# One graph-network kernel, one edit: the running maxima are subtracted by VectorE instead of by a matrix product, and the weighting runs two steps behind the scores

## What is computed

```python
for i in range(NUM_BLOCKS):                      # 4
    y = _cond_layer_norm(x, cond, ...)
    # _sparse_attention, H = 4 heads of Dh = 128
    q = (x @ wq + bq).reshape(N, H, Dh) * Dh ** (-0.5)
    k = (x @ wk + bk).reshape(N, H, Dh)
    v = (x @ wv + bv).reshape(N, H, Dh)
    scores = jnp.einsum('ehd,ehd->eh', q[src], k[dst])
    smax = jax.ops.segment_max(scores, src, num_segments=N)
    ex = jnp.exp(scores - smax[src])
    denom = jax.ops.segment_sum(ex, src, num_segments=N)
    attn = ex / denom[src]
    out = jax.ops.segment_sum(attn[:, :, None] * v[dst], src, num_segments=N)
    x = x + (out.reshape(N, D) @ wo + bo)
    ...                                          # conditional norm and perceptron
```

## Time and profile before

| | us |
|---|---|
| median of 3 runs | 3189.87 |
| lowest and highest run | 3188.07, 3192.56 |
| the profiled execution, its own time | 3188.7 |
| its span (first to last instruction) | 3186.9 |
| PE busy in it | 2920.2 (92%) |
| DVE busy | 1862.6 (58%) |
| POOL busy | 898.7 (28%) |
| ACT busy | 793.4 (25%) |

### The profile page before, as it was taken

How to read it: one execution, slowest core, us unless ns; L and a number is a source line. 1 busy time by engine, 2 the same in 40 slices (tenths; PEclk the granted TensorE clock), 3 DMA queues, 4 the chain that set the end, 5 groups by cost and what they waited for, 6 DMA issues and landing times.

```text
span 3186.9 us, 32021 instructions
## 1 busy us (share of the span) xinstructions
PE 2920.2 (92%) x11830; PEld 1894.8 (59%) x11830; DVE 1862.6 (58%) x3327; ACT 793.4 (25%) x1145; POOL 898.7 (28%) x730
## 2 busy tenths in 40 slices
PE   5878899999899999899999899999967799899999
PEld 1345567776457776457777456777534456566555
DVE  9999755556734555855554765554765788503111
ACT  1154442223112223112222212222221212213221
POOL 6632413344113343223333222334420500000100
PEclk9989899999999999999999999999988899999999
DMA  3000110001400000400000410000253144101001
GB/s 80 17 7 1 40 53 0 27 1 44 119 20 1 1 27 34 114 21 14 1 27 14 116 40 14 1 27 1 92 142 102 40 131 140 56 4 63 14 1 33
DMA packets 69063, 133.70 MB, mean 42 GB/s; under 512 B 10804, under 2 KB 11195, under 8 KB 68908
## 3 DMA queue, kind: packets, MB, share of 16 engines
q1 hardware_dynamic: 63372, 119.62, 12.7%
q0 software_dynamic: 5536, 12.03, 1.2%
HBM read 120.70 MB, written 10.92 MB: 41 GB/s over the span
## 4 chain that ended last, share of the span: by engine, by line
PE 76%; DVE 13%; DMA 4%; DVEq 2%; issue 2%; ACT 1%; POOLq 1%; POOL 1%; SPq 0%; ACTq 0%
PE ps L1504 12%; PE ps L1616 10%; PE ps L1731 9%; PE ps L1760 9%; PE ps L1495 7%; PE ps L1658 4%; PE ps L1589 3%; PE ps L1604 3%; PE ps L1606 3%; PE ps L1607 3%; PE ps L1605 3%; PE ps L1457 2%; PE ps L1752 2%; PE ps L1521 2%; DVE onehot_src L895 2%; DMA lite_ring<-in_basis 2%
## 5 line engine op out<-in xcount | busy, mean ns | idle before, releaser
L687 POOL TENSOR_TENSOR pacc<-pacc,prob 125x628 f32<-125x628 f32 (+1 forms) x288 | 406.5, 1411 | 381.4 <-DVE prob L1024 381.4
L1504 PE MATMUL ps<-yT,w 128*128 128x416 f32 (+1 forms) x1152 | 437.3, 536 | 18.8 <-DVE qk_lo L961 11.6
L970 DVE CUSTOM_DVE_ANT_0 ps<-ps,typed 125x628 f32<-125x628 f32 x320 | 260.2, 824 | 234.0 <-PE ps L1589 233.5
L1616 PE MATMUL ps<-prob,big 125*128 125x314 f32 x1280 | 392.5, 428 | 4.6 <-DVE prob L1024 4.6
L1327 ACT ACTIVATE prob<-ps 125x628 f32<-125x628 f32 x320 | 221.9, 693 | 630.9 <-PE ps L1607 630.9
L1760 PE MATMUL ps<-pieces,counts_r 125*125 125x512 f32 x1400 | 353.8, 407 | 1.7 <-DVEq L1120 1.6
L1504 PEld LDWEIGHTS ps<-yT,w 128*128 128x128 f32 x1152 | 225.9, 198 | 204.9 <-issue 193.1
L1024 DVE SCALAR_TENSOR_TENSOR prob<-prob,typed 125x628 f32<-125x628 f32 x320 | 260.0, 812 | 122.7 <-ACT prob L1327 122.7
L1760 PEld LDWEIGHTS ps<-pieces,counts_r 125*125 125x125 f32 x1400 | 257.1, 186 | 79.3 <-issue 17.4
L1604 PE MATMUL ps<-qk_hi 128*125 128x314 f32 x640 | 293.9, 459 | 0.1
L1616 PEld LDWEIGHTS ps<-prob,big 125*128 125x128 f32 x1280 | 228.2, 190 | 60.5 <-DVE prob L1024 9.2
(11 more groups left out here) (207 smaller groups left out, 4602.1 us busy)
## 6 DMA issues: line engine op xcount, KB each, us to landing
lite_ring<-in_basis SPq DMA_DIRECT2D x120, 256.0 KB, 2.7
basis<-in_basis SPq DMA_DIRECT2D x120, 256.0 KB, 2.6
w<-in_m_w SPq DMA_DIRECT2D x8, 1024.0 KB, 6.7
w<-in_wk SPq DMA_DIRECT2D x5, 1024.0 KB, 5.5
oT<-in_cw SPq DMA_DIRECT2D x9, 512.0 KB, 6.2
w<-in_wv SPq DMA_DIRECT2D x4, 1024.0 KB, 5.9
w<-in_wq SPq DMA_DIRECT2D x4, 1024.0 KB, 6.5
w<-in_wo SPq DMA_DIRECT2D x4, 1024.0 KB, 5.5
```

The source lines that it names most:

```text
L687: nc.gpsimd.tensor_tensor(pacc[:, c0:c0 + nn], pacc[:, c0:c0 + nn], prob[:, n % 3, p0:p0 + nn], ALU.add).then_inc(psum_done, 1)
L970: V.tensor_tensor_reduce(out=score_ps(s.slot), in0=score_ps(s.slot), in1=in_quarters(mneg[:, t, c0:c0 + HALF]), scale=1.0, scalar=-BIG, op ...
L1504: last = mm(lin_ps(job, 128, nn), weight[:, k, m * 128:(m + 1) * 128], lhs[:, k, c0:c0 + nn], start=(k == 0), stop=(k == KD - 1))
L1616: last = mm(o_halves[:, b, :], vrow[:, t, h * DH:(h + 1) * DH], prob[:, n % 3, b * QUARTER:(b + 1) * QUARTER], start=(t == 0), stop=(t == ...
```

## The change

Steps of the weighting pass are divided in two kinds. In "subtracted" steps (all of head 3, the lower steps of heads 1 and 2, and every other step, with j odd, of the rest) the fourth product of each quarter is left out, and a new DVE instruction (`shift_scores`, a TENSOR_TENSOR) adds minus the maxima to the tile while it moves it from PSUM to `prob`. ACT then takes the exponential in place in `prob`. There are 10 such steps in head 0, 15 each in heads 1 and 2, and 20 in head 3: 60 of 80 per block, 240 in all.

For that, minus the maxima must stand in every row: `max_row` now multiplies with `nmx[:, t]` broadcast to 125 columns, so that its product has 125 equal rows, and ACT copies 125 rows instead of 1 into `shift` (before: `mrow`). The steps that keep the fourth product use a matrix whose first row alone is ones.

DVE does `shift_scores` of step j + 1 at the head of its step j, ahead of `masked_max`, of the product with the counts and of `add_out`. PE weights step j - 2 instead of j - 1 in step j. A slot of a subtracted tile is free when DVE has shifted it (`shifted`).

```diff
--- before.py
+++ after.py
@@ -175,6 +175,18 @@
 SCORES = {(s.kind, s.h, s.j): s for s in plan_scores()}
 SCORES_PER_BLOCK = len(SCORES)
 EXPS = MAXES = HEADS * 2 * T
+
+
+def subtracted(h, j):
+    return h == HEADS - 1 or (h > 0 and j < T) or j % 2 == 1
+
+
+SHIFT_NO = {}
+for _h in range(HEADS):
+    for _j in range(2 * T):
+        if subtracted(_h, _j):
+            SHIFT_NO[_h, _j] = len(SHIFT_NO) + 1
+SHIFTS = len(SHIFT_NO)
 
 
 def build(nc, a, out):
@@ -292,6 +304,7 @@
         hi_ready = sem("hi_ready")
         score_full = sem("score_full")
         exp_done = sem("exp_done")
+        shifted = sem("shifted")
         max_done = sem("max_done")
         neg_max_ready = sem("neg_max_ready")
         prob_ready = sem("prob_ready")
@@ -398,14 +411,14 @@
         junk = pacc[:].bitcast(F16)[:, 0:N]
         cw = sl("cw", [128, 4, D], F32R)
         stage = oT[:, 0:2 * D].rearrange("p (a d) -> p a d", d=D)
-        mrow = sl("mrow", [128, N], F32R)
+        shift = sl("shift", [P, N], F32R)
         bcol = sl("bcol", [128, 3, KD], F32)
         mxp = sl("mxp", [P, T, 2], F32)
         nmx = sl("nmx", [P, T], F32R)
         mx = sl("mx", [P, T], F32)
         ident_r = sl("ident_r", [P, P + 1], F32R)
         rden = sl("rden", [P, T], F32)
-        ones_r = sl("ones_r", [128, 128], F32R)
+        first_row = sl("first_row", [P, P], F32R)
         att.close()
         keep.close()
 
@@ -875,12 +888,12 @@
 
             dve.wait_ge(edge_placed, EC)
             V.tensor_copy(es[:].rearrange("p a s -> p (a s)"), o_ps[:, 0:2 * SLOTS])
-            V.memset(ones_r[:].bitcast(F32), 1.0)
-            V.memset(mrow[:].bitcast(F32), 0.0)
+            V.memset(first_row[:].bitcast(F32), 0.0)
             V.memset(condS[:, N:N + 2].bitcast(F32), 0.0)
             V.memset(ident_r[:].bitcast(F32), 0.0)
             V.drain()
             V.tensor_copy(ident_r[:, 0:P], ident[0:P, 0:P])
+            V.memset(first_row[0:1, :].bitcast(F32), 1.0)
             V.drain().then_inc(blk_done, 1)
 
             for g in range(GROUPS):
@@ -1011,13 +1024,29 @@
                     V.scalar_tensor_tensor(out=x[:, t, :], in0=lin_ps(job, P, D), scalar=rden[:, t:t + 1],
                                            in1=x[:, t, :], op0=ALU.mult, op1=ALU.add).then_inc(lin_empty[job.slot], 1)
 
+                def shift_scores(h, j):
+                    s, n = SCORES["exp", h, j], h * 2 * T + j
+                    c0 = HALVES[j // T]
+                    dve.wait_ge(score_full, at(i, SCORES_PER_BLOCK, s.n + 1))
+                    if n >= 3:
+                        dve.wait_ge(pv_done, at(i, EXPS, n - 2))
+                        dve.wait_ge(psum_done, at(i, EXPS, n - 2))
+                    V.tensor_tensor(in_quarters(prob[:, n % 3, :]), score_ps(s.slot),
+                                    in_quarters(shift[:, c0:c0 + HALF].bitcast(F32)), ALU.add).then_inc(shifted, 1)
+
                 for h in range(HEADS):
                     if h == 1:
                         dve.wait_ge(xbias_done, at(i, 2, 1))
+                    for job in g["mrow"][h][-2:]:
+                        dve.wait_ge(lin_empty[job.slot], job.emptied)
                     for j in range(2 * T):
 
                         n = h * 2 * T + j
                         t, c0, nn = j % T, HALVES[j // T], HALF
+                        if j == 0 and subtracted(h, 0):
+                            shift_scores(h, 0)
+                        if j + 1 < 2 * T and subtracted(h, j + 1):
+                            shift_scores(h, j + 1)
                         if h + 1 < HEADS:
                             masked_max(h + 1, j)
                         dve.wait_ge(exp_done, at(i, EXPS, n + 1))
@@ -1286,8 +1315,8 @@
                     for n, job in enumerate(g["mrow"][h]):
                         t0, t1 = 4 * n, min(4 * n + 4, T)
                         act.wait_ge(lin_full, job.full)
-                        A.activation(mrow[0:1, t0 * P:t1 * P].rearrange("o (t n) -> o t n", n=P),
-                                     lin_ps(job, 1, (t1 - t0) * (P + 1)).rearrange("o (t n) -> o t n", n=P + 1)[:, :, 0:P],
+                        A.activation(shift[:, t0 * P:t1 * P].rearrange("o (t n) -> o t n", n=P),
+                                     lin_ps(job, P, (t1 - t0) * (P + 1)).rearrange("o (t n) -> o t n", n=P + 1)[:, :, 0:P],
                                      ACT.Copy).then_inc(lin_empty[job.slot], 1)
 
                 def copy_o(h, half):
@@ -1320,11 +1349,17 @@
                 for h in range(HEADS):
                     for j in range(2 * T):
                         s, n = SCORES["exp", h, j], h * 2 * T + j
-                        act.wait_ge(score_full, at(i, SCORES_PER_BLOCK, s.n + 1))
-                        if n >= 3:
-                            act.wait_ge(pv_done, at(i, EXPS, n - 2))
-                            act.wait_ge(psum_done, at(i, EXPS, n - 2))
-                        A.activation(in_quarters(prob[:, n % 3, :]), score_ps(s.slot), ACT.Exp, scale=DH ** -0.5).then_inc(exp_done, 1)
+                        if subtracted(h, j):
+                            act.wait_ge(shifted, at(i, SHIFTS, SHIFT_NO[h, j]))
+                            scores = prob[:, n % 3, :]
+                        else:
+                            act.wait_ge(score_full, at(i, SCORES_PER_BLOCK, s.n + 1))
+                            if n >= 3:
+                                act.wait_ge(pv_done, at(i, EXPS, n - 2))
+                                act.wait_ge(psum_done, at(i, EXPS, n - 2))
+                            scores = score_ps(s.slot)
+                        to = prob[:, n % 3, :] if subtracted(h, j) else in_quarters(prob[:, n % 3, :])
+                        A.activation(to, scores, ACT.Exp, scale=DH ** -0.5).then_inc(exp_done, 1)
                         if j == T:
                             copy_o(h, 0)
                     if h + 2 < HEADS:
@@ -1577,7 +1612,10 @@
                         if b.kind == "max":
                             pe.wait_ge(max_done, at(i, MAXES, b.h * 2 * T + b.j + 1))
                         else:
-                            pe.wait_ge(exp_done, at(i, EXPS, b.h * 2 * T + b.j + 1))
+                            if subtracted(b.h, b.j):
+                                pe.wait_ge(shifted, at(i, SHIFTS, SHIFT_NO[b.h, b.j]))
+                            else:
+                                pe.wait_ge(exp_done, at(i, EXPS, b.h * 2 * T + b.j + 1))
 
                 def max_scores(h, j):
 
@@ -1603,8 +1641,9 @@
                         o = score_ps(s.slot)[:, b, :]
                         mm(o, hi[:, 1, rows], hi[:, 0, cols], start=True, stop=False)
                         mm(o, hi[:, 1, rows], lo[:, 0, cols], start=False, stop=False)
-                        mm(o, lo[:, 1, rows], hi[:, 0, cols], start=False, stop=False)
-                        last = mm(o, ones_r[:, 0:P], mrow[:, cols], start=False, stop=True)
+                        last = mm(o, lo[:, 1, rows], hi[:, 0, cols], start=False, stop=subtracted(h, j))
+                        if not subtracted(h, j):
+                            last = mm(o, first_row[:], shift[:, cols], start=False, stop=True)
                     last.then_inc(score_full, 1)
 
                 def weighted_values(h, j):
@@ -1625,7 +1664,7 @@
                         tiles = range(4 * n, min(4 * n + 4, T))
                         for t in tiles:
 
-                            last = mm(lin_ps(job, 1, P + 1, (t - 4 * n) * (P + 1)), nmx[:, t:t + 1], ident_r[:],
+                            last = mm(lin_ps(job, P, P + 1, (t - 4 * n) * (P + 1)), nmx[:, t:t + 1].to_broadcast([P, P]), ident_r[:],
                                       start=True, stop=True)
                         last.then_inc(lin_full, 1)
 
@@ -1665,14 +1704,15 @@
                             if j == 0:
                                 projected(h + 1)
                             max_scores(h + 1, j)
-                        if j:
-                            weighted_values(h, j - 1)
+                        if j >= 2:
+                            weighted_values(h, j - 2)
                         if h and j < T:
                             if j == 0:
                                 pe.wait_ge(o_copied, at(i, 2 * HEADS, 2 * h))
                                 if h == 1:
                                     pe.wait_ge(w_in[0], at(i, 32, 32))
                             attended(h - 1, j)
+                    weighted_values(h, 2 * T - 2)
                     if h + 2 < HEADS:
                         project(h + 2, 0)
                     weighted_values(h, 2 * T - 1)
```

## The result

The changed kernel takes 3497.57 us (median of 4 runs, 3486.52 to 3543.48) against 3191.22 for the kernel before. One execution, the 3543 us one, was slow: TensorE's granted clock stood at 0.949 in it where it is otherwise 1.00 (0.915 in the mean, against 0.960 to 0.963), and it is left out of the ratio, 1.0945 [1.0919, 1.097]. Run again unedited (e1_again) it took 3488.39 (3486.70 to 3496.15), a ratio of 1.0935 [1.0917, 1.0953]. The forecast was 3476.

A forecast was written before the change was run, and what follows sets the result against it. PE, 76% of the chain, bounds the kernel, streaming unbroken in attention. Per block, waits for DVE net of savings add 71.8 us (head 0 16.6, heads 1 and 2 45.6 - 0.5, head 3 8.5, `max_row` 1.6): 3188.7 + 287 = 3476 us, range 3425 to 3525.

The forecast's parts named there:

- PE waits for the maximum in 152 steps: Heads 0 to 2, before the maximum scores: 152 PE gaps of about 1.95 us, some 295 us in all.
- Periods: Attention steps: lower steps of heads 1 and 2 5.02 us instead of 3.37; head 3 lower 4.28, upper 2.04.
- Pairs: Two steps with one shift, head 0 and upper steps of heads 1 and 2: 6.66 us instead of 5.00.
- Head 3's output products: Head 3's lower steps: PE waits for the output sum queued behind the shift, 32 gaps of about 1.5 us.
- What goes, 69 us: 240 steps lose two products of 0.144 us each: 69 us of PE time, a gain if DVE answered in time.
- `max_row`, 6 us: Ten products per head load 125 columns instead of 1: 0.4 us per head, 6 us in all.
- The lag: PE weighting two steps behind the scores: no wait forecast for it; a weighting moved into head 2's end gap gives -0.5 us.
- head 0's: Head 0's share of a block's sum: ten pairs at 1.66 us, 16.6 us, before its max_row share.
- such spells: Extra half clock at the heads' ends, 0 to 2 spells per block: up to 14 us more, in the range only.
- rival 1: TensorE's clock falls in every second of 46 waits per block: 161 us more, 3637 us; chance 0.05.
- rival 2: Head 3 does not wait, its output sums come in time: 32 steps less 1.5 us, 3428 us; chance 0.04.
- rival 3: PE never waits for DVE, so the 69 us become a gain: 3120 us; chance 0.03.

The follow-up runs named there:

- e2: The changed kernel with the maximum of step j put ahead of the shift of step j + 1 on DVE: 3299.11 us, ratio 1.0331.
- e4: The changed kernel with both maximum and output sum ahead of the shift in DVE's queue: 3166.67 us, ratio 0.9925 to the kernel before.
- e3: The changed kernel with the output sum of step j - 1 ahead of the shift, the maximum still behind it: 3440.45 us, ratio 1.0786.
- e7: The kernel before without the fourth product in the same 240 steps and nothing in its place: 3125.55 us, ratio 0.9792.
- e8: The kernel before with only the 125 equal rows of max_row added: 3198.1 us, ratio 1.0018.
- e5: The kernel before with only the lag: PE weights two steps behind the scores instead of one: 3222.07 us, ratio 1.0096.
- e12b: The changed kernel with only ACT's copy of the output's first half one step later: 3497.08 us, ratio 1.095.
- e10b: The changed kernel with maximum and output sum ahead of the shift, and ACT's copy of the output's first half one step later: 3171.23 us, ratio 0.9936.

## Why the prediction was right

- **PE waits for the maximum in 152 steps: right in place, count and size.** 295 us were forecast and 296.5 measured, in 152 waits. The step that carries the forecast, DVE's order at a point where both engines need each other, is proved by e2 and e4: the order alone is worth 189 us, and 322 with the output sum's.
- **Periods.** Lower steps of heads 1 and 2: 5.02 forecast, 5.02 and 5.03 measured. Pairs: 6.66 and 1.53 + 5.16 = 6.69. Head 3 lower 4.28 forecast and 4.27 measured, upper 2.04 and 2.03 to 2.05. The new instruction took 0.81, and 0.73 to the next start, as read from the maximum. The estimate from the Trainium skill ("Perfetto Trace Analysis", Optimizing Scalar/DVE Operations) was 0.78 from start to start; the trace has 0.73 here too.
- **Head 3's output products.** Right: in its lower steps PE waits for L1024, as in this timeline of PE in block 0, and e3 removes this wait alone: 48 us, as 32 gaps of 1.5 us had been forecast.

```profile
767.90 1.22 PE L1655 MATMUL ps<-prob,big 125*128 125x314 f32 x4
770.34 1.12 PE L1697 MATMUL ps<-w,oT 128*125 128x512 f32 x2 [1.23 <-DVE x L1024]
```

- **What goes, 69 us.** 66 by e7.
- **`max_row`, 6 us.** Partly luck. e8 measured 6, but the wide products themselves cost 0.27 us a head, 4 us in all, and longer spells of half clock the rest. Their busy time grew as bounded: 27.0 us for the 160 against 18.5.
- **The lag was costed at nothing, and that was wrong by itself.** It costs 30 us alone (e5), 20 of them through ACT's queue, which I had not followed past the copy. The sum did not suffer, since the slot of step 11 is freed by DVE's shift in the changed kernel, and so the late exponential doesn't hold PE (e12b, and e10b where no other wait covers it). The forecast had not looked at this, so that was luck.
- **The miss: 3476 against 3488.** Per block 71.8 were forecast and 75.0 measured: head 0 17.0 and 20.1, heads 1 and 2 together 45.9 and 46.5, head 3 8.9 and 8.4 (each with its share of `max_row`). So the term at fault is head 0's, and what it lacks is time at half clock. Head 0 has 10.2 us of it in each block, against 3.4 in the kernel before, and 6.8 us more at half clock lose some 3.4 us. Without these, block 1 would come to 71.6 us by this estimate, and 71.8 were forecast. Where the spells lie differs. In block 0 all is at the head's end. Timeline of PE there:

```profile
540.66 4.32 PE L1728 MATMUL ps<-ones_f,pacc 125*125 125x1 f32 x20 [0.46 <-ACT shift L1318]
```

and the stretches around it (columns as in the earlier trace rows):

```profile
540.70:544.10 3.40, 3.40 (x17) 3.40 (x17) 0.00 (x0) 0.17 (x1) 0.00 (x0) 0.50 0.00 0
...
547.50:550.90 3.40, 3.40 (x6) 1.69 (x5) 0.00 (x0) 0.13 (x1) 0.00 (x0) 0.50 0.00 0
550.90:554.30 3.40, 3.40 (x14) 2.08 (x12) 0.65 (x1) 1.04 (x2) 0.00 (x0) 0.99 0.00 0
```

The clock is at 0.50 from 540.7 to 550.9, 10.2 us. Before, it was there for one stretch of 3.4 us, and the denominators' products still ran at full clock. The kernel before, timeline of PE:

```profile
526.41 2.34 PE L1688 MATMUL ps<-ones_f,pacc 125*125 125x1 f32 x20 [0.55 <-ACT mrow L1289]
```

and its stretches:

```profile
526.40:529.90 3.50, 3.48 (x24) 3.00 (x25) 0.39 (x2) 0.22 (x1) 0.00 (x0) 1.00 0.02 5
529.90:533.30 3.40, 3.40 (x7) 1.63 (x6) 0.00 (x0) 0.00 (x0) 0.00 (x0) 0.50 0.00 0
```

The twenty denominators' products took 4.32 us instead of 2.34, and the sixteen projections behind them 8.87 instead of 7.53: 3.3 us. In blocks 1 to 3 the end loses only half of that (in block 1 the same products take 2.94 and 8.60 us), and the other spell of 3.4 us stands in the steps, right behind the first of PE's waits for the maximum. The stretches of block 1:

```profile
1035.70:1039.10 3.40, 1.61 (x12) 1.53 (x11) 3.25 (x7) 0.73 (x1) 0.91 (x1) 1.00 0.00 0
1039.10:1042.50 3.40, 3.40 (x10) 2.65 (x10) 1.00 (x1) 0.69 (x1) 1.84 (x2) 0.50 0.00 0
```

Two steps of PE there take 3.45 + 4.71 us, against 2.34 + 4.19 in block 0. The forecast had up to 14 us for such spells, at the heads' ends, in its range and none in its sum; over the whole kernel 269 us at half clock instead of 246 cost 12 by this estimate, the distance from 3476 to 3488. What drew the longer spells is not settled. e4 has the wide rows and the lag as well, and head 0 has no more half clock there than in the kernel before; its longer spells stand at the ends of heads 1 and 2.

- **Rivals.** The clock (rival 1) stays at 1.00 in all steps of heads 1 and 2, and the mean is 0.962 as before. But it fell once in the steps of head 0 in three of four blocks, where the kernel before has no fall: 5 us in all, where the rival had 161. Head 3 did wait (rival 2). PE did wait (rival 3); in e4, with nearly all of these waits gone, the kernel is faster than before.

## What to carry to other kernels

An instruction added to an engine with slack is costed by its place in that engine's queue, not by its length: ask what the other engine needs next, and put that first. Here the same instructions in another order took 3.08 us in a lower step of heads 1 and 2 instead of 5.02, and the kernel went from 9.35% slower to 0.75% faster. When a consumer is moved a step later, follow every queue that waits for it, down to the odd instruction that runs once in twenty steps, and then ask which event frees the buffer at its end: the same late copy cost 20 us where the exponential freed the score slot, and nothing where the shift did. And a total that comes out as forecast doesn't prove the term: the 6 us of e8 were 4 us of products and a longer spell of half clock.
